# Join of batches and layer norms of the cross attention in pieces; bias on another engine; last join and the norms round the feed-forward stage rearranged

## The reference, cut to what matters

```python
x0 = layernorm(x)                                  # no gain, no shift
h  = layernorm(mha(x0, x0, causal) + x0) * g1 + be1
h  = layernorm(h + mha(h, ctx))          * g2 + be2   # ctx: 8 x 1601 x 512, 16 heads of 32, value bias bv2
f  = relu(h @ Wf1 + bf1) @ Wf2 + bf2                  # 512 -> 2048 -> 512
x1 = x + layernorm(h + f) * g3 + be3
n1 = layernorm(x1)                                 # goes into the next part (delta rule)
```

## Time and profile before

| what | value |
|---|---|
| median of 3 runs | 1663.97 us (1660.92 to 1666.47) |
| the profiled execution, its own time | 1666.27 us |
| its span, first to last instruction | 1664.7 us |
| mean granted clock of TensorE, share of full | 0.948 |
| busy: TensorE, VectorE, ScalarE, GpSimd | 91%, 56%, 40%, 15% |
| cross rounds, in the span | about 152 to 1017 us |
| feed-forward stage | about 1017 to 1121 us |

### The profile page before, as it was taken

The page is one execution under the profiler, slowest core; times in us unless marked ns, Lnnn a source line. Parts: engine busy times, 40 slices in busy tenths (PEclk is TensorE's granted clock), DMA queues, the critical chain, the costliest instruction groups (busy, mean ns, idle before and its releaser), DMA issues.

```text
span 1664.7 us, 28092 instructions
## 1 busy us (share of the span) xinstructions
PE 1522.0 (91%) x11828; PEld 1172.9 (70%) x11828; DVE 932.5 (56%) x1381; ACT 671.1 (40%) x1223; POOL 256.2 (15%) x169
## 2 busy tenths in 40 slices
PE   7859999999999999999988885996999689999998
PEld 3547988888777887778877774872499376666665
DVE  4482343434554445544365535437776668888885
ACT  1114443344333433433444542432321236666664
POOL 1003221111111011110112232202152200000000
PEclk9969999999999999999999996997889779999999
DMA  7001211110101101010111228006000019999992
GB/s 258 1 0 55 70 49 42 39 43 20 42 21 39 33 30 42 21 39 25 38 43 40 69 80 313 14 5 223 0 1 27 0 53 346 329 345 343 347 339 96
DMA packets 86779, 163.13 MB, mean 98 GB/s; under 512 B 4608, under 2 KB 27136, under 8 KB 86144
## 3 DMA queue, kind: packets, MB, share of 16 engines
q1 hardware_dynamic: 86656, 161.34, 28.2%
HBM read 160.28 MB, written 1.05 MB: 97 GB/s over the span
## 4 chain that ended last, share of the span: by engine, by line
PE 83%; DVE 11%; issue 2%; ACT 1%; POOL 1%; DMA 0%; DVEq 0%; ACTq 0%; POOLq 0%
PE ring L601 18%; PE ring L591 15%; PE ring L1801 8%; PE turnbank L635 6%; PE pv L1825 4%; PE sc L618 3%; PE pv L654 3%; PE sc L1466 3%; PE sc L1079 3%; PE pv L1801 3%; PE pv L1833 2%; PE sc L1489 1%; PE ring L1088 1%; PE pv L663 1%; DVE nm L827 1%
## 5 line engine op out<-in xcount | busy, mean ns | idle before, releaser
L559 POOL TENSOR_TENSOR x_l<-raw,x_h 128x1536 fp32r<-128x1536 f32 (+1 forms) x44 | 160.1, 3640 | 693.7 <-ACT x_h L553 693.7
L1650 DVE TENSOR_TENSOR w_lo<-w_raw,w_hi 128x2048 fp32r<-128x2048 f32 x88 | 200.4, 2284 | 25.1 <-ACT w_hi L1891 25.0
L744 ACT ACTIVATE prob<-sc,nm 128x384 f32<-128x384 f32 (+1 forms) x256 | 153.9, 611 | 119.5 <-DVE nm L832 80.7
L601 PE MATMUL ring<-wv_h,x_h 128*128 128x512 f32 (+2 forms) x520 | 192.0, 369 | 0.0
L591 PE MATMUL ring<-x_h,wk_h 128*128 128x384 f32 (+1 forms) x512 | 186.3, 364 | 5.4 <-POOL x_l L559 5.4
L827 DVE TENSOR_REDUCE nm<-sc 128x2 f32<-128x898 f32 (+1 forms) x128 | 127.8, 1020 | 105.2 <-PE sc L618 105.1
L601 PE MATMUL ring<-wv_h,x_l 128*128 128x512 f32 (+2 forms) x520 | 182.2, 350 | 0.0
L601 PE MATMUL ring<-wv_l,x_h 128*128 128x512 f32 (+2 forms) x520 | 182.1, 350 | 0.0
L591 PE MATMUL ring<-x_h,wk_l 128*128 128x384 f32 (+1 forms) x512 | 176.8, 345 | 0.0
L591 PE MATMUL ring<-x_l,wk_h 128*128 128x384 f32 (+1 forms) x512 | 176.3, 344 | 0.0
L1891 ACT CAST w_hi<-w_raw 128x2048 fp32r<-128x2048 f32 x88 | 167.6, 1907 | 18.4 <-PE pv L1825 15.5
(11 more groups left out here) (447 smaller groups left out, 2758.2 us busy)
## 6 DMA issues: line engine op xcount, KB each, us to landing
w_raw<-in_ew SPq DMA_DIRECT2D x96, 1024.0 KB, 5.4
raw<-in_ctxT SPq DMA_DIRECT2D x33, 768.0 KB, 4.4
raw<-in_ctxT SPq DMA_DIRECT2D x11, 900.0 KB, 4.7
wf<-in_wf SPq DMA_DIRECT2D x2, 4096.0 KB, 19.0
xin<-in_x SPq DMA_DIRECT2D x1, 1024.0 KB, 5.6
w_in<-in_wq SPq DMA_DIRECT2D x1, 1024.0 KB, 7.8
w_in<-in_wk SPq DMA_DIRECT2D x1, 1024.0 KB, 10.1
w_in<-in_wv SPq DMA_DIRECT2D x1, 1024.0 KB, 12.2
```

Source lines behind the costliest of these rows:

```text
L559: pool.tensor_tensor(x_l[x % 3][:, :, 0:w], raw[x % 3][:, :, 0:w], x_h[x % 2][:, :, 0:w].bitcast(F32), ALU.subtract)\
L601: m = pe.matmul(ring[k % 2][0:rows, 0:cols.stop - cols.start], xt[:, c, t1:t1 + rows], wt[:, c, cols], start=c == 0 and n == 0, stop=c == ...
L744: act.activation(prob[:, i, 0:WIDTHS[r]], sc[:, i, score_columns(r)], ACT.Exp, bias=nm[:, b % 2, r, h:h + 1], accum_out=psum[:, b % 2, r, ...
L1650: return eng.tensor_tensor(w_lo[n % NSLOT][:, :, :], w_raw[n % NSLOT][:, :, :], w_hi[i % 4][:, :, :].bitcast(F32), ALU.subtract)
```

## The change

In the cross rounds:

- The bias bv2 is added to all four tiles by one GpSimd operation ahead of the rounds' splits; VectorE's add per tile goes. The first join add waits for it (`bias_added`).
- The join of a finished batch spreads over two rounds: factors and scale in the first round of the next batch, behind the first two turned copies (scale ahead of slot 3), the add in the second, behind the jobs of slot 0 and ahead of the mix. ScalarE's exponential moves from the end of the old batch into the first round of the next.
- The norm of tiles 0 to 2 is in two pieces: statistics ahead of slot 2, centre ahead of slot 3.
- In the last batch the shift is taken a round earlier; the sums, factors, scale and add of the first three head groups come before the last mix, and only the fourth group is left after it.

Round the feed-forward stage:

- Tile 3's norm comes ahead of the first two weight splits. `hidden(0)` waits for each chunk of the turned x by itself.
- be3 is added to `xres` for all tiles at once, so that one operation applies the norm's scale and adds both.
- The last norm's application moves to ScalarE, as x * rstd + nshift; GpSimd forms nshift = -mean * rstd with two more operations per tile.

```diff
 def pool_cross(pool, link):
     for x in range(6):
         pool_split(pool, x)
+    pool.wait_ge(sem("rows_loaded"), 64)
+    pool.wait_ge(sem("turned"), 2)
+    pool.tensor_tensor(xa[:, :, :], xa[:, :, :], over_tiles(bv2[:, :]), ALU.add).then_inc(sem("bias_added"), 1)
...
 def act_cross(act):
...
             if more:
                 act_exp(act, n + 1, 0)
                 act_exp(act, n + 1, 1)
+            else:
+                act_join(act, B - 1)
...
                 act_exp(act, n + 1, 3)
+            if n % 8 == 0 and n > 0:
+                act_join(act, n // 8 - 1)
             act_jobs(act, PLAN[n][1])
...
-            if n % 8 == 7:
-                act_join(act, n // 8)
...
 def dve_cross(dve, link):
...
-            joins = n % 8 == 0 and n > 0
+            joins, every = n % 8 < 2 and n >= 8, range(0, 4)
             dve_turned(dve, n, last_turn(n))
             if more:
                 dve_max(dve, link, n + 1)
             dve_jobs(dve, PLAN[n][0])
-            if joins:
-                dve_join_factors(dve, link, b - 1)
-            if n % 2:
-                dve_mix(dve, link, n // 2)
-            elif more:
+            if joins and n % 2:
+                dve_join_add(dve, link, b - 1, every).then_inc(sem("cross_added"), 1)
+            if n == NR - 1:
+                dve_denominators(dve, link, n // 2)
+                dve_join_factors(dve, link, b)
+                dve_join_scale(dve, link, b, range(0, 3))
+                link(dve_join_add(dve, link, b, range(0, 3)))
+                dve_mix(dve, link, n // 2)
+            elif n % 2:
+                dve_denominators(dve, link, n // 2)
+                dve_mix(dve, link, n // 2)
+            else:
                 dve_shift(dve, n + 1)
             if more:
                 dve_turned(dve, n + 1, 0)
-            if joins:
-                dve_join_scale(dve, link, b - 1)
             dve_jobs(dve, PLAN[n][1])
             if more:
                 dve_turned(dve, n + 1, 1)
-            if joins:
-                dve_join_add(dve, link, b - 1)
+            if joins and n % 2 == 0:
+                dve_join_factors(dve, link, b - 1)
+            if n in X_B:
+                dve_x_b_stats(dve, link, X_B.index(n))
             dve_jobs(dve, PLAN[n][2])
             if more and n % 2 == 0:
                 dve_turned(dve, n + 1, 2)
+            if n in X_B:
+                dve_x_b_center(dve, link, X_B.index(n))
+            if joins and n % 2 == 0:
+                dve_join_scale(dve, link, b - 1, every)
             dve_jobs(dve, PLAN[n][3])
-            if n % 8 == 7:
+            if n % 8 == 7 and more or n == NR - 2:
                 dve_join_shift(dve, link, b)
-            if n in X_B:
-                dve_x_b(dve, link, X_B.index(n))
             if n - 1 in X_B:
                 dve_x_b_end(dve, X_B.index(n - 1))
-        dve_join_factors(dve, link, B - 1)
-        dve_join_scale(dve, link, B - 1)
-        dve_join_add(dve, link, B - 1)
+        dve_join_scale(dve, link, B - 1, range(3, 4))
+        dve_join_add(dve, link, B - 1, range(3, 4)).then_inc(sem("cross_added"), 1)
...
 def dve_ffn(dve, link):
+        dve_x_b_stats(dve, link, NT - 1)
+        dve_x_b_center(dve, link, NT - 1)
+        dve_x_b_end(dve, NT - 1)
         split(0)
         split(1)
-        dve_x_b(dve, link, NT - 1)
-        dve_x_b_end(dve, NT - 1)
...
         link(dve.tensor_tensor(xa[:, :, :], xa[:, :, :], over_tiles(bf2[:, :]), ALU.add))
+        link(dve.tensor_tensor(xres[:, :, :], xres[:, :, :], over_tiles(rows3[:, 1, :]), ALU.add))
...
-        for t in range(NT + 1):
-            if t < NT:
-                link(norm_shift(dve, 3, tmp, tmp, t, rows3[:, 1, :]))
-                link(dve.tensor_tensor(xa[:, t, :], tmp[:, t, :], xres[:, t, :], ALU.add))
-                norm_stats(dve, link, xa, t)
-            if t >= 1:
-                norm_apply(dve, 4, tmp, xa, t - 1).then_inc(sem("normed"), 1)
+        for t in range(NT):
+            link(norm_shift(dve, 3, xa, tmp, t, xres[:, t, :]))
+            norm_stats(dve, link, xa, t)
...
+    def act_last_norm(act):
+        for t in range(NT):
+            act.wait_ge(sem("shift_scaled"), t + 1)
+            act.activation(tmp[:, t, :], xa[:, t, :], ACT.Identity, scale=rstd[:, t:t + 1], bias=nshift[:, t:t + 1])\
+               .then_inc(sem("normed"), 1)
...
 def pe_ffn(pe):
-        pe.wait_ge(sem("turned_copied"), 12)
...
             for c in range(NC):
+                if m == 0:
+                    pe.wait_ge(sem("turned_copied"), 8 + c + 1)
...
 def pool_delta(pool, link):
-        for n in (3, 4):
-            for t in range(NT):
-                norm_rstd(pool, link, n, t)
+        for t in range(NT):
+            norm_rstd(pool, link, 3, t)
+        for t in range(NT):
+            norm_rstd(pool, link, 4, t)
+            pool.wait_ge(sem("rstd_ready"), norm_count(4, t))
+            link(pool.tensor_tensor(nshift[:, t:t + 1], mv[:, t, 0:1], rstd[:, t:t + 1], ALU.mult))
+            pool.tensor_scalar(nshift[:, t:t + 1], nshift[:, t:t + 1], -1.0, None, ALU.mult).then_inc(sem("shift_scaled"), 1)
```

More of the change, by code:

```diff
@@ L70, in build @@
     rstd = at("rstd", 1216, [P, NT])
+    nshift = at("nshift", 1888, [P, NT])
     mhalf = at("mhalf", 1248, [P, 64])
@@ L839, in dve_shift, with dve_denominators @@
            .then_inc(sem("shift_ready"), 1)
-    def dve_mix(dve, link, g):
+    def dve_denominators(dve, link, g):
         b, c = g // 4, g % 4
         hs = slice(4 * c, 4 * c + 4)
-        mixed = mix[:, c * P:(c + 1) * P].rearrange("p (h e) -> p h e", h=4)
-        folded = pv[:, 2 * P:4 * P].rearrange("p (r h e) -> p r h e", r=2, h=4)
         dve.wait_ge(sem("corr_ready"), g + 1)
@@ L850, in dve_mix @@
         link(dve.tensor_tensor(den[:, b % 2, hs], den[:, b % 2, hs], psum[:, b % 2, 1, hs], ALU.add))
+    def dve_mix(dve, link, g):
+        b, c = g // 4, g % 4
+        mixed = mix[:, c * P:(c + 1) * P].rearrange("p (h e) -> p h e", h=4)
+        folded = pv[:, 2 * P:4 * P].rearrange("p (r h e) -> p r h e", r=2, h=4)
         dve.wait_ge(sem("cross_folded"), g + 1)
-        link(dve.tensor_tensor(mixed, folded[:, 0, :, :], over_width(corr[:, b % 2, hs], E), ALU.mult))
+        link(dve.tensor_tensor(mixed, folded[:, 0, :, :], over_width(corr[:, b % 2, 4 * c:4 * c + 4], E), ALU.mult))
         dve.tensor_tensor(mixed, folded[:, 1, :, :], mixed, ALU.add).then_inc(sem("group_mixed"), 1)
@@ L873, in dve_join_factors, with dve_join_scale, dve_join_add @@
         link(dve.tensor_tensor(jf[:, 0, :], jf[:, 0, :], jf[:, 2, :], ALU.mult))
[L875 to L881, removed]
+    def dve_join_scale(dve, link, b, groups):
+        hs = slice(4 * groups.start, 4 * groups.stop)
+        mixed = mix[:, :].rearrange("p (h e) -> p h e", h=H)[:, hs, :]
+        dve.wait_ge(sem("group_mixed"), 4 * b + groups.stop)
+        link(dve.tensor_tensor(mixed, mixed, over_width(jf[:, 0, hs], E), ALU.mult))
+    def dve_join_add(dve, link, b, groups):
         k, t = b % 2, b // 2
         r, o = slice(k * S, k * S + S), slice(S - k * S, P - k * S)
-        link(dve.tensor_copy(cat[r, :], mix[o, :]))
-        link(dve.tensor_tensor(cat[r, :], cat[r, :], mix[r, :], ALU.add))
-        dve.tensor_tensor(xa[r, t, :], xa[r, t, :], cat[r, :], ALU.add).then_inc(sem("cross_added"), 1)
+        cols = slice(groups.start * P, groups.stop * P)
+        link(dve.tensor_copy(cat[r, cols], mix[o, cols]))
+        link(dve.tensor_tensor(cat[r, cols], cat[r, cols], mix[r, cols], ALU.add))
+        if b == 0:
+            dve.wait_ge(sem("bias_added"), 1)
+        return dve.tensor_tensor(xa[r, t, cols], xa[r, t, cols], cat[r, cols], ALU.add)
     def dve_cross(dve, link):
@@ L996, in split_views, with dve_x_b_stats @@
         return hid[:, k, :], hid_h[:, k, :], hid_l[:, k, :]
-    def dve_x_b(dve, link, t):
+    def dve_x_b_stats(dve, link, t):
         dve.wait_ge(sem("cross_added"), 2 * (t + 1))
@@ L1002, in dve_x_b, with dve_x_b_center @@
             dve.wait_ge(sem("rows2_loaded"), 32)
-        link(dve.tensor_tensor(xa[:, t, :], xa[:, t, :], bv2[:, :], ALU.add))
         norm_stats(dve, link, xa, t)
+    def dve_x_b_center(dve, link, t):
         dve.wait_ge(sem("variance_ready"), norm_count(2, t))
@@ L1975, in _ @@
         act_ffn(act)
+        act_last_norm(act)
         act_delta(act)
```

## The result

The changed kernel takes 1659.78 us in the median of 15 runs (1656.6 to 1662.84), the kernel before 1663.18 beside it (15 runs, 1659.95 to 1666.47). The ratio is 0.9979, 95% interval 0.997 to 0.9989: 3.5 us less, between 1.8 and 5.0. The forecast was 2.1 us less, at 1661.9. The measured difference is clear of zero but inside the 0.3% that the prediction named as what a measurement of this kernel can tell, and the time is inside its range. A second comparison on another occasion gave 0.9977 (0.9967 to 0.9987).

What follows compares the result with a forecast made beforehand. TensorE, busy 91% of the span, was taken as the bound, so only its gaps counted; -6.7 - 1.5 + 2.2 - 1.3 - 0.7 + 4.2 + 1.7 = -2.1 us gave 1661.9 us, 8-in-10 range 1655 to 1667.5.

Steps and rivals of the forecast that it cites:

- Last join: Hand-over to feed-forward: only the last group's columns remain between last mix and tile 3's statistics; 5.7 us saved.
- First product without four chunks: Start of feed-forward: first product starts after the first xb_l piece instead of all four; 1.85 us saved.
- Second wide add: Ahead of first down product: another 2.29 us VectorE add delays the split; 0.85 us lost, leaving 6.7 of 7.55.
- End norms: After the feed-forward stage: shorter VectorE work, apply on ScalarE, last transposes start earlier; 1.5 us saved, bounds 0 and 3.2.
- Bias on GpSimd: Round 1: GpSimd's 4.6 us add holds a VectorE minimum, making TensorE wait; 2.2 us lost, bounds 0 and 2.6.
- bv2 out of the norms: Rounds 19, 35, 51: VectorE's bias add goes, but the centre still queues behind GpSimd's split; worth 0.
- Rival (b): Norm centres in rounds 19, 35, 51 beat GpSimd's split, three gaps of 1.6 us vanish: 1657.1 us, chance 0.10.
- Join over two rounds: Cross rounds: factors behind turned copies save 1.3 us, moved exponential 0.7; the add in odd rounds loses 4.2.
- rival (c): Join's add in odd rounds lies on the path in all seven, 13.3 us instead of 4.2: 1671.0 us, chance 0.08.
- Clock: Cross rounds: after new TensorE gaps of 1.5 us or more, one stretch at lower clock; 1.7 us lost.
- Rival (a): Gaps in the rounds stay away: GpSimd's add doesn't catch VectorE, no clock falls: 1658.0 us, chance 0.22.
- Rival (d): Shortened feed-forward ends don't shorten: low clock leaves 5.1 of 6.7, GpSimd's chain eats the norms' gain: 1665.0 us, chance 0.10.

Runs made afterwards that it cites:

- e1: Kernel before with only the shortened last join and the other hand-over edits into the feed-forward stage (tile 3's bias in round 26): median 1658.46 us, ratio 0.997.
- e7: Repeat of e1, the kernel before with the shortened last join alone: median 1657.74 us, ratio 0.9959.
- e9: Changed kernel with VectorE applying the last norm again and GpSimd's two extra operations per tile gone: median 1659.12 us, ratio 0.998.
- e10: Changed kernel with the norm's shift column made by one VectorE operation per tile instead of GpSimd's two, ScalarE still applying: median 1657.78 us, ratio 0.9973.
- e5: Changed kernel with statistics and centre of the norms of tiles 0 to 2 moved up behind the round's first turned copy: median 1653.04 us, ratio 0.9935.
- e4: Changed kernel with the join's add back in the even round, behind its last copy: median 1653.34 us, ratio 0.9948.
- e2: Kernel before with only the end norms changed (wide be3 add, one-operation shift, last apply on ScalarE): median 1660.56 us, ratio 0.9992.
- e6: Changed kernel with bias back on VectorE, join's add in the even round, and norm statistics and centre early: median 1645.45 us, ratio 0.9887.

## Why the prediction was right

The median came 2.1 us below the forecast. The places of the waits were named rightly; that the total lies so near is in part luck, for terms were missed on both sides, and as measured they make 5.0 less, where the forecast had 2.1 and the times show 3.5. They came out as follows, in the order of the prediction.

**Last join, 5.7 saved:** 7.0 to 1.26 us, so 5.7. **First product without four chunks, 1.85:** with the join 7.44 measured, 7.55 said. No run separates these two terms. **Second wide add, 0.85 lost:** TensorE waited 0.73 us for VectorE's split, and 6.80 was left of the 6.7 forecast. But the add itself cost 0.1 us and not 0.85: from first hidden to first down product e1 and e7, which lack it, take 8.36 and 8.30 us, and every kernel that has it behind the shortened join 8.46, behind VectorE. Another 0.5 went to TensorE itself: it needed 7.82 for this piece in the trace of before, at a granted clock of 0.69, and had 0.64 and 0.65 there in e1 and e7. So VectorE does set the time, as said, but most of the loss isn't the add's, and that 6.7 and 6.8 agree so well is luck.

**End norms, 1.5 saved:** measured 2.2. The place was right (GpSimd is the last releaser of all four applies), the term was mis-sized. GpSimd took 7.1 us from its first to its last operation of the four tiles (1131.43 to 1138.57) where the prediction had 7.9, 1131.1 to 1139.0: VectorE's shifts held it up by less than the 1.8 assumed. And the prediction treated the four parts as one edit. e9 and e10 show what this hid: the operation saved is worth 2.9, and ScalarE's part takes 0.7 of it back. I had priced ScalarE's apply at 0.65 us by VectorE's copy; it took 0.81, and as the last apply is on the path, these 0.16 us count in full, against the statement that a tenth changes nothing.

**Bias on GpSimd, 2.2 lost:** 2.18 (that length was 14.27 before), with the 4.6 us operation and the held minimum as said. The Trainium skill's page "SBUF — State Buffer", section "Who interferes with whom", has the second one to issue fully blocked until the first is finished; the 3.51 us of the minimum, which takes 0.16 alone and ends 0.02 behind GpSimd's add, agree. The prediction says that the trace has no case of VectorE issuing first. It has one, ahead of the rounds; timeline of the kernel before:

```profile
128.82 2.29 DVE L303 TENSOR_TENSOR wv_l<-wv,wv_h 128x2048 fp32r<-128x2048 f32 x1
129.83 4.57 POOL L559 TENSOR_TENSOR x_l<-raw,x_h 128x1536 fp32r<-128x1536 f32 x1 [8.18 <-ACT x_h L553]
```

VectorE, 1.0 us ahead, keeps its 2.29 us, and GpSimd's split takes 4.57 in place of 3.46. e5 is no such case, for there the centre has ended 2.3 us before the split starts.

**bv2 out of the norms, 0:** the gaps are 1.54, 1.61 and 1.53, before 1.54 to 1.60. Rival (b) needed the centre ahead of the split; it came 0.30, 0.30 and 0.14 us too late, so that the gaps stayed; e5 moved it ahead by 3.3. By how little it could be ahead and still escape no run shows.

**Join over two rounds, 1.3 and 0.7 saved:** round 56 gave 1.09 and round 48 0.33, 1.4 in all. Rounds 16 and 32 gave 0.62 each and rounds 8, 24 and 40 0.1, 1.5 in all, where 0.7 was forecast for the moved exponential. Here the term was too small: in rounds 16 and 32 a wait of 0.20 for a turned copy vanished as well, which I hadn't counted. No run moves the exponential alone, so its share isn't shown. **4.2 lost:** 1.65, 1.79 and twice 0.64, so 4.7, in the four rounds named and in no other; rival (c) falls. e4 gives 3.9 of it back, and 0.8 of round 49's stays.

**Clock, 1.7 lost:** the prediction counted one such stretch behind a new gap. In the changed kernel's own two traces there is none. But e5 and e9, with the same code in round 1, have one behind the wait of 1.90 us, worth 1.55 us: two of six traces. So the mechanism is real and a whole one was too much, 0.5 us on average by these few traces. Elsewhere in the rounds the lengths with half clock sum to 1.9 us less in the changed kernel's trace than in the one of before. But e2, with before's code in the rounds, took 847.4 us where before took 850.4, so a difference of this size is spread of the same code, and nothing about the change.

The measured terms make -6.8 - 2.2 + 2.2 - 1.4 - 1.5 + 4.7 = -5.0 us. Two comparisons gave 3.5 and 3.8 less, each with an interval that reaches 5. The stretch at half clock in round 1, where it comes, takes a part of the difference. Whether more is lost in stages that the change doesn't touch stays open; the spread of start and rest hides it. Rival (a), the gaps in the rounds stay away, is false in its mechanism, though its time (1658.0) is as near as the forecast's. Rival (d) falls with the two hand-overs.

So why did a change with 11.9 us of gain by its traces, 9.0 of it at the two hand-overs, give 3.5? It paid 2.2 for a bias add that had been free on VectorE, 4.7 for moving the join's add into rounds where a copy waits behind it, and it left three gaps of 1.6 us one step away from vanishing. Undone or moved, these are worth 10.8 us in the lengths that the edits touch and 13 to 15 in time (e6).

## What to carry to other kernels

Before an operation moves, list what stands behind its new place in the same queue and who waits for that: the same 1.9 us of work cost nothing in six even rounds and 0.8 us in the seventh, and 1.65 and 1.79 us in rounds 49 and 57. A wide GpSimd operation on SBUF is not free just because GpSimd is idle; look for the VectorE operations with two SBUF inputs that come while it runs, and let them start ahead of it, by reordering if need be. Here such an operation was held whether it came 0.14 or 1.0 us behind. Split a several-part edit of a chain into its parts before you call it a gain: here ScalarE's apply lost 0.7 us with its scalar column from GpSimd and gained 0.5 with the column from VectorE.

## What the runs showed of the hardware

- A VectorE minimum on 128x2 elements took 3.51 us beside GpSimd's add on 128x2048, in place of 0.16. With VectorE ahead by 1.0 us, GpSimd's split of 128x1536 took 4.57 us in place of 3.46 and VectorE's subtraction its 2.29.
- ScalarE's Identity with a scale and a bias column took 0.81 us for 128x512, in all four tiles and in e2 and e10; VectorE's form with two columns took 0.51 to 0.55.
- With VectorE through, GpSimd's operations on 128x1 took 0.19 to 0.24 us with 0.08 between them, its power 0.56. While VectorE worked with two inputs in SBUF they took up to 0.78, the power up to 1.04.
- The same code at the start took 150.0 to 157.1 us. Between the changed kernel and e9 the difference is nearly all in TensorE's busy time at a different granted clock, as these windows show (busy PE 120.17 and 115.53 us for the same 552 instructions, granted clock 0.85 and 0.88 in the column behind POOL). Over all traces the mean clock there was 0.82 to 0.89:

```profile
0.00:157.06 157.06, 120.17 (x552) 80.78 (x553) 79.42 (x124) 31.35 (x45) 19.31 (x30) 0.85 0.21 72
```

```profile
0.00:152.10 152.10, 115.53 (x552) 76.52 (x553) 79.31 (x124) 31.37 (x45) 19.27 (x30) 0.88 0.22 74
```
